# Edge stage: DVE makes the low parts of the weight pieces behind the mask of the scanned logits instead of in front of the scan

## The reference, cut to what matters

```
e     = leaky_relu(a_src[src] + a_dst[dst], 0.2)      # one logit per edge and head
emax  = segment_max(e, dst);  ee = exp(e - emax[dst])
alpha = ee / segment_sum(ee, dst)[dst]
agg   = segment_sum(h[src] * alpha, dst)              # the edge stage computes this
x     = x + gnn_ffn(layer_norm(agg + xn @ W_res + bias))
x     = x + top-2 of 8 experts: gelu(xn @ W1[e] + b1) @ W2[e] + b2
```

## Time and profile before

| | |
|---|---|
| median of 3 runs | 2294.04 us (2293.52 to 2295.35) |
| profiled execution | 2291.67 us, of which the span from first to last instruction 2290.4 us |
| granted TensorE clock, mean of the span | 0.856 of full speed |
| busy, share of the span: PE / DVE / ACT / POOL | 78% / 76% / 68% / 52% |

### The profile page before, as it was taken

How to read it: one execution, slowest core, us unless ns; L and a number is a source line. 1 busy time by engine, 2 the same in 40 slices (tenths; PEclk the granted TensorE clock), 3 DMA queues, 4 the chain that set the end, 5 groups by cost and what they waited for, 6 DMA issues and landing times.

```text
span 2290.4 us, 43652 instructions
## 1 busy us (share of the span) xinstructions
PE 1796.5 (78%) x12962; PEld 1538.9 (67%) x12962; DVE 1745.3 (76%) x5414; ACT 1556.3 (68%) x3225; POOL 1184.8 (52%) x1168
## 2 busy tenths in 40 slices
PE   6537666676666677766666899999399999999998
PEld 4425545555545455555544788889399999999997
DVE  7349999899899899989998788887455555555554
ACT  3366777777677777676772787887377766666675
POOL 3377777777777777777770134445222222222223
PEclk9857777777777777777777999999699999999999
DMA  7867666767666667766664223322835356436432
GB/s 228 209 184 215 215 210 197 207 216 215 214 205 203 208 214 215 225 200 200 204 207 136 74 91 98 101 78 75 253 48 122 48 118 159 87 48 158 85 48 38
DMA packets 283231, 358.12 MB, mean 156 GB/s; under 512 B 118629, under 2 KB 227006, under 8 KB 280562
## 3 DMA queue, kind: packets, MB, share of 16 engines
q1 hardware_dynamic: 218578, 202.63, 28.7%
q0 software_dynamic: 63840, 151.61, 26.0%
q10 hardware_dynamic: 576, 1.09, 0.2%
HBM read 464.93 MB, written 95.79 MB: 245 GB/s over the span
## 4 chain that ended last, share of the span: by engine, by line
PE 46%; POOL 21%; issue 11%; DVE 11%; ACT 6%; DMA 4%; DVEq 0%; SPq 0%; POOLq 0%; ACTq 0%
POOL edge_mem L768 21%; PE bank L1156 8%; PE bank L1144 7%; PE bank L1145 7%; PE bank L1146 7%; PE bank L957 6%; PE bank L1155 4%; DMA edge_mem<-node_table,src_col 3%; ACT edge_mem L862 3%; DVE layer_rounded L1140 1%; PE bank L1153 1%; ACT edge_mem L868 1%; DVE edge_mem L1023 1%; PE bank L523 1%; PE bank L834 1%
## 5 line engine op out<-in xcount | busy, mean ns | idle before, releaser
L768 POOL DMA_INDIRECT edge_mem<-node_table,src_col x880 | 840.5, 955 | 277.2 <-issue 261.7
L957 PE MATMUL bank<-edge_mem 128*128 128x264 f32 x1760 | 524.1, 459 | 6.3 <-ACT edge_mem L897 3.3
L957 PEld LDWEIGHTS bank<-edge_mem 128*128 128x128 f32 x1760 | 382.9, 226 | 110.1 <-issue 26.3
L1886 POOL DMA_INDIRECT out<-expert_mem,slot_tok x112 | 174.4, 1557 | 488.4 <-DVE expert_mem L1823 468.5
L1873 ACT ACTIVATE expert_mem<-bank,par 128x256 f32<-128x256 f32 x448 | 221.8, 495 | 187.6 <-PE bank L1146 187.5
L1140 DVE TENSOR_TENSOR expert_rounded<-expert_mem,expert_rounded 128x512 fp32r<-128x512 f32 x280 | 193.6, 691 | 194.6 <-ACT expert_rounded L1873 121.9
L1023 DVE TENSOR_TENSOR edge_mem<-edge_mem,bank 128x1056 f32<-128x1056 f32 x385 | 293.9, 776 | 7.5 <-ACT bank L889 1.7
L1156 PE MATMUL bank<-expert_rounded 128*128 128x512 f32 x784 | 278.8, 395 | 0.0
L1144 PE MATMUL bank<-expert_rounded 128*128 128x256 f32 x896 | 254.6, 284 | 27.1 <-DVE expert_rounded L1140 27.1
L862 ACT ACTIVATE edge_mem<-iota,dst_col 128x128 bf16<-128x128 bf16 x880 | 262.8, 386 | 0.0
L1145 PE MATMUL bank<-expert_rounded 128*128 128x256 f32 x896 | 254.4, 284 | 0.0
(11 more groups left out here) (245 smaller groups left out, 4240.6 us busy)
## 6 DMA issues: line engine op xcount, KB each, us to landing
expert_rounded<-split_w SPq DMA_DIRECT2D x114, 2048.0 KB
edge_mem<-step_place SPq DMA_DIRECT2D x55, 512.0 KB, 5.4
split_w<-piece_hi SPq DMA_DIRECT2D x72, 256.0 KB, 4.8
split_w<-piece_lo SPq DMA_DIRECT2D x72, 256.0 KB, 6.0
piece_full<-in_L_ffn_W SPq DMA_DIRECT2D x64, 256.0 KB
expert_mem<-expert_rows SPq DMA_DIRECT2D x224, 64.0 KB, 2.8
edge_mem<-node_table,src_col POOLq DMA_INDIRECT x880
node_table<-win_mem SPq DMA_DIRECT2D x12, 544.0 KB, 4.4
```

Source lines behind the costliest of these rows:

```text
L768: pool.indirect_dma_start(gath[g % NGB][:, t, :], None, node_table, bass.IndirectOffsetOnAxis(ap=src_col[:, k, t % 2:t % 2 + 1], axis=0)). ...
L957: ins = pe.matmul(bank[4 + at % 3][:, 0:AGG], onehot[g % 2][:, 2 * k + j, :], gath[g % NGB][:, 2 * k + j, 0:AGG], start=(j == 0), stop=(j ...
```

## The change

In the loop of `edges_dve` the low parts of group n's pieces, which stood in front of the waits of the scan, stand behind the mask, and so in front of the scores of group g. No instruction is added or left out, and the other engines' programs are the same.

```diff
                 if n < NG:
-                    for i in pieces_of(n):
-                        low_piece(i)
                     dve.wait_ge(asrc_turned, n + 1)
                     dve.wait_ge(seg_loaded[n % 2], 32 * (n // 2 + 1))
                     if n >= 1:
...
                     dve.tensor_tensor_scan(seg_max[:, :], seg_new[n % 2][:, :], b_asrc[0:HEADS * GS, 0:EB], -BIG, ALU.add, ALU.max).then_inc(scanned, 1)
                     dve.wait_ge(scanned, n + 1)
                     dve.tensor_tensor(seg_max[:, :], seg_max[:, :], seg_last[n % 2][:, :], ALU.mult).then_inc(masked, 1)
+                    for i in pieces_of(n):
+                        low_piece(i)
                 if 0 <= g < NG:
                     gb = gath[g % NGB]
```

## The result

The changed kernel takes 2301.77 us (median of 10 runs, 2297.88 to 2308.2) against 2293.61 us for the kernel before (10 runs): ratio 1.0038, 95% interval 1.0027 to 1.0048. The forecast was 2294.0 with a range to 2298.0; the time lies outside, on the side of rival B. The profiled execution took 2300.96 us, its span is 2299.7, 9.3 us longer than before.

The account below looks back on a forecast made before the run. POOL's unbroken walk through the gathers bounds the edge stage. Profiled 2291.67 us + 0 (POOL's walk) + 0 (tail) = 2291.7; the runs' median is 2.4 us above that execution, so 2294.0, range 2290.5 to 2298.

Parts of the forecast that it names:

- rival B: Edge stage, slower: low parts fall into step with gathers, each holding one by half the maximum; +9 us, 2303; chance 0.05.
- POOL paces the stage: Edge stage: POOL issues one gather per 1.25 us with 0.305 us gaps and never waits for another engine.
- The chain inside a group: DVE in a group: scores come 0.65 us sooner, some 0.6 waited again at cand_rest; 0.1 us phase gain, not adding up.
- Rival A: Edge stage, faster: DVE paces it, so saved low-part waits are won, at most 38.9 us; 2255; chance 0.05.
- D: DVE's low parts still wait as long, since DVE comes earlier by what it saved; time 2294; chance 0.03.
- The stretch: Gather time above 880 x 0.946 us, 8.0 us before: moved low parts leave the sum unchanged, spread 1.3 us.
- outer bound of +26.2: Upper end for lengthened gathers: each of 72 low parts stretches one by the maximum 0.475 us, less 8.0 us.
- The tail: After the last gather: earlier DVE only waits longer for ACT, stage still ends 48.06 us behind that gather; gain zero.

Follow-up runs that it names:

- e2: Changed kernel with the low parts one place further back, behind the scores and in front of cand_rest: 2297.8 us, ratio 1.0016 to the kernel before.
- e3: Kernel before plus one unused instruction of the mask's size, two SBUF inputs, behind each group's low parts: 2297.86 us, ratio 1.0019.
- e10: Kernel before with only SP's load of the last group's places made to wait for the last gathers' landing: 2291.78 us, ratio 0.9984.
- e11: e2 plus the extra unused instruction of e3, put directly in front of each group's low parts: 2307.89 us, ratio 1.0057 to the kernel before.
- e5: Changed kernel with each low part also waiting for the end of the mask and of the previous low part: 2296.39 us, ratio 1.0012.
- e1: Changed kernel plus a small DVE copy from PSUM in front of each low part: 2304.85 us, ratio 1.0051 to the kernel before.
- e8: Changed kernel with SP's load of the last group's places waiting for the last gathers' landing: 2297.38 us, ratio 1.0014 to the kernel before.
- e4: Changed kernel with each low part cut to 8 of its 512 columns: 2287.96 us, ratio 0.9978 to the kernel before.
- after_again: The changed kernel measured once more, unaltered: 2301.64 us, ratio 1.0029 to the kernel before.

## Why the prediction was wrong, step by step

**POOL paces the stage: right.** The gaps of 0.305 us did not change in any kernel, and DVE's saved waits bought nothing. The spans follow the stretch and the tail: from the end of the stage to the end of the span it is 1037.1 to 1039.0 us in eleven of the fourteen profiles, and 1040.8, 1040.7 and 1035.6 in e2, e3 and e10.

**The chain inside a group: right.** The low parts' wait fell from 42.5 to 28.8 - 7.0 = 21.8 us without the longest (forecast 10 to 20, so just above), cand_rest's new wait is 35.5 us (forecast 15 to 35), DVE's busy time 971.02 us (970.66). Rival A is refuted, and D too.

**The stretch, taken as 0 with a spread of 1.3 us: the step that failed.** It measured +6.6 us in the recorded execution and +10.5 in the second one, inside the outer bound of +26.2 but far outside the spread. Two assumptions broke. First, I carried the mean cost of a low part over to another place because no fixed beat was in sight. What a low part costs POOL depends on what stands in front of it: with the mask in front and no pause between, a gather can be held past the mask and the low parts, or past both low parts of a pair. e11 shows it by adding such an instruction elsewhere, e5 by putting a pause in its place: none is over 1.5 us, and the time falls by 5.2 us. And all 57 gathers over 1.5 us in the five profiles that have such an instruction in front and no added waits (both of the changed kernel, e1, e8, e11) stand in groups where DVE did not pause between it and the low part. Second, I took the longest gather, 1421 ns, for the most that a low part can do. That was the most in the old order, and the new one went to 2198. Rival B had the sign and, with +9 us, the size, but its mechanism only in part: not a fixed step with the gathers at half the old maximum, but nine to twelve gathers held for much longer. More of them meet a low part too (32 to 40 in the orders with the mask in front, 24 before), but so do 33 in e2, whose stretch is that of before; why they are more is open.

The rule of the Trainium skill (SBUF — State Buffer, Who interferes with whom), that a DVE instruction with two SBUF inputs contends with a GpSimd instruction that reads SBUF, was the one to lean on: e4 agrees with it, with 12.8 of 14.6 us gone when the low parts are short. Its own bound in the prediction, one instruction's 0.69 us per gather, was too small as well: 1.25 us was measured.

**The tail, taken as zero: off by 2.35 us**, and by 1.6 in after_again. I took the landing of the last gather for given. DVE's earlier phase frees SP earlier, and its loads then run ahead of the last gather; e8 shows that SP's loads delay the landing. The prediction named SP's queue but looked only at the pieces' stores in it.

**Not settled:** why a short instruction with two SBUF inputs holds a gather on from in front of a low part and not from behind; e3 and e11 rule out the total length of the run as the cause, e1 rules out that the two must touch. Also which of SP's loads delays the last gather, and where the differences behind the stage in e2, e3 and e10 come from.

## What to carry to other kernels

When POOL issues gathers without a pause, a DVE instruction with two SBUF inputs can be on its path, though no wait in the profile says so: look at the spread of POOL's own instruction (median, maximum, sum over the median) before moving such work. Taking a wait away from a DVE that is not the bound can cost time, since the wait was also the gap in which POOL got in; where such work can't be avoided, short instructions issued one by one cost less (a stretch of 4.9 against 8.0 us here). And an engine that comes early lets loads go early: see what they land in front of.

## What was not expected of the hardware

A gather of 0.946 us lasted up to 2.39 us (e1) behind DVE work; a 0.15 us instruction on PSUM between two such instructions did not let it in, a wait of 0.1 us for the semaphore of the one in front did (e5, none over 1.46 us). And the order decides: the same short instruction in front of the low parts lets 18 gathers grow over 1.5 us (e11), behind them none (e3).
